# The dispatch scatters of a mixture-of-experts layer, paced by their landings

## The reference

```python
def _moe_forward(x, Wg, W1, W3, W2, Ws1, Ws3, Ws2):
    xt = x.reshape(-1, D)                                  # 2048 tokens x 512
    scores = jax.nn.softmax(xt @ Wg.T, axis=-1)
    ...                                                    # the best 2 of 4 groups, then the best 4 experts
    topi = jax.lax.top_k(masked, TOPK)[1]
    weights = jnp.take_along_axis(scores, topi, axis=1) * ROUTE_SCALE
    combine = jnp.zeros((T, E), xt.dtype).at[jnp.arange(T)[:, None], topi].add(weights)
    h = jax.nn.silu(jnp.einsum('td,eid->eti', xt, W1)) * jnp.einsum('td,eid->eti', xt, W3)
    expert_out = jnp.einsum('eti,edi->etd', h, W2)
    y = jnp.einsum('etd,te->td', expert_out, combine)
    z = jax.nn.silu(xt @ Ws1.T) * (xt @ Ws3.T) @ Ws2.T     # the shared experts
    return (y + z).reshape(B, S, D)
```

## Time and profile before

| what | value |
|---|---|
| median of 3 runs | 1945.23 us (1937.94 to 1947.1) |
| the profiled execution's own time | 1941.7 us |
| its span, first to last instruction | 1940.0 us |
| PE busy | 1519.6 us, 78% of the span |
| DVE busy | 1094.2 us, 56% |
| POOL busy | 685.1 us, 35% |
| ACT busy | 624.9 us, 32% |
| mean granted TensorE clock | 0.895 |

### The profile page before, as it was taken

How to read it: one execution, slowest core, us unless ns; L and a number is a source line. 1 busy time by engine, 2 the same in 40 slices (tenths; PEclk the granted TensorE clock), 3 DMA queues, 4 the chain that set the end, 5 groups by cost and what they waited for, 6 DMA issues and landing times. The chain is left out here.

```text
span 1940.0 us, 29164 instructions
## 1 busy us (share of the span) xinstructions
PE 1519.6 (78%) x9516; PEld 703.0 (36%) x9525; DVE 1094.2 (56%) x1809; ACT 624.9 (32%) x1103; POOL 685.1 (35%) x685
## 2 busy tenths in 40 slices
PE   1778787877167888888888748607999999999987
PEld 1344443434012222222222125203555555556443
DVE  6444444444568888988898376402344444444376
ACT  4312120303225666656666743001111111111121
POOL 3000000000545333333320024660364645666274
PEclk9989898998656899999999958858999999999999
DMA  4251607080344312222120012350566556573365
GB/s 173 55 195 36 214 14 235 0 249 8 105 126 138 66 34 47 53 47 47 28 56 1 1 47 93 151 195 11 180 177 157 163 146 173 159 200 87 114 189 179
DMA packets 183543, 211.00 MB, mean 109 GB/s; under 512 B 89968, under 2 KB 135600, under 8 KB 182960
## 3 DMA queue, kind: packets, MB, share of 16 engines
q1 hardware_dynamic: 154224, 123.73, 23.8%
q0 software_dynamic: 18592, 66.99, 11.1%
q10 hardware_dynamic: 10656, 19.40, 2.6%
HBM read 101.09 MB, written 88.87 MB: 98 GB/s over the span
## 5 line engine op out<-in xcount | busy, mean ns | idle before, releaser
L804 DVE TENSOR_REDUCE ca_mx<-ca_sc 128x1 f32<-128x512 f32 x512 | 327.6, 677 | 86.7 <-PE ca_sc L724 86.1
L77 PE MATMUL re_ab<-fx_w,re_xt 128*128 x1800 | 295.7, 314 | 10.9 <-DMA re_xt<-slot_rows 10.6
L937 ACT ACTIVATE ca_pt<-ca_st 128x512 f32<-128x512 f32 x512 | 264.5, 596 | 101.1 <-PE ca_st L736 101.1
L724 PE MATMUL ca_sc<-ca_ks,ca_qs 48*128 48x512 f16 x512 | 190.4, 424 | 53.7 <-DVE ca_mx L804 29.2
L77 PEld LDWEIGHTS re_ab<-fx_w,re_xt 128*128 128x128 f16 x1800 | 173.3, 98 | 109.0 <-issue 14.6
L736 PE MATMUL ca_st<-ca_qs,ca_ks 49*128 49x512 f16 x512 | 172.4, 400 | 40.6 <-ACT ca_pt L937 34.7
L77 PE MATMUL re_yp<-fx_w,re_ht 128*128 (+1 forms) x666 | 156.0, 379 | 0.0
L478 POOL TENSOR_TENSOR sa_yt<-sa_yf,sa_yt 128x512 f16<-128x512 f32 x16 | 18.5, 1156 | 385.8 <-ACT sa_yt L461 385.8
L1484 POOL TENSOR_TENSOR fx_w<-re_raw_w,fx_w 128x272 f16<-128x272 f32 x224 | 153.9, 723 | 1.7
L749 PE MATMUL ca_pv<-ca_pt,ca_va 128*32 128x512 f32 x1024 | 148.6, 645 | 1.0 <-DVE ca_turned L817 0.5
L77 PE MATMUL sh_yp<-sh_pair,sh_ht 128*128 128x512 f16 (+1 forms) x288 | 78.3, 430 | 77.6 <-DVE x_sb L1205 64.1
(11 more groups left out here) (236 smaller groups left out, 2432.3 us busy)
## 6 DMA issues: line engine op xcount, KB each, us to landing
re_raw_w<-in_we POOLq DMA_DIRECT2D x56, 544.0 KB, 4.6
slot_rows<-sa_zeros SPq DMA_DIRECT2D x12, 1792.0 KB, 16.0
slot_outs<-re_ys ACTq DMA_DIRECT2D x74, 256.0 KB, 2.0
sa_scratch<-sa_qk SPq DMA_DIRECT2D x16, 512.0 KB, 4.4
ca_scratch<-ca_qk SPq DMA_DIRECT2D x64, 128.0 KB, 1.8
sa_qs<-sa_scratch SPq DMA_DIRECT2D x12, 512.0 KB, 6.5
sa_ks<-sa_scratch SPq DMA_DIRECT2D x12, 512.0 KB, 6.8
ca_qs<-ca_scratch SPq DMA_DIRECT2D x48, 128.0 KB, 3.7
```

Of the source, the lines that this page charges most:

```text
L77: last = nc.tensor.matmul(out, lhs(a, c), rhs(b, c), start=(c == 0 and n == 0), stop=(c == chunks - 1 and n == len(PRODUCTS) - 1))
L724: nc.tensor.matmul(sc[:, m % RING, :], qs[rows, c % SLOTS, pair, qt * P:(qt + 1) * P], ks[rows, c % SLOTS, pair, :], start=True, stop=True ...
L804: nc.vector.reduce_max(mx[:, qd // 4, qd % 4, 2 * a + jj:2 * a + jj + 1], sc[:, m % RING, :], AX.X).then_inc(maxed, 1)
L937: nc.scalar.activation(pt[:, (4 * qd + k) % 8, :], st[:, m % RING, :], ACT.Exp, scale=SCALE).then_inc(exp_done, 1)
```

## The change

Two semaphores replace the one, and are used in turn. From the third scatter on, each waits until the scatter two places in front of it has landed (a landing adds 16). Two scatters at most are so under way at a time. At the end GpSimd waits for both counts. Nothing else is changed: size, order and number of the scatters are the same.

```diff
--- before.py
+++ after.py
@@ -1206,6 +1206,9 @@
                                      ALU.add).then_inc(self.added, 1)
 
 
+ABREAST = 2
+
+
 def route_and_share(nc, split, sems, ident, x_sb, xn, rows, route, wg_dram, we_dram, slot_rows, first_pairs):
 
 
@@ -1250,7 +1253,8 @@
         packed = sb("packed", [1, TILES], F32)
         made, logits_ready, shifted, exped, chain = (
             sem("made"), sem("logits_ready"), sem("shifted"), sem("exped"), sem("chain"))
-        masks_ready, placed, routed, sent = sem("masks_ready"), sem("placed"), sem("routed"), sem("sent")
+        masks_ready, placed, routed = sem("masks_ready"), sem("placed"), sem("routed")
+        sent = [sem(f"sent{n}") for n in range(ABREAST)]
         block = ctx.enter_context(nc.Block())
 
         @block.sync
@@ -1276,11 +1280,15 @@
                 shared.low_part(pool, nc.gpsimd, n)
 
             pool.wait_ge(routed, 1)
-            for t, k in sends:
+            for m, (t, k) in enumerate(sends):
+                if m >= ABREAST:
+                    pool.wait_ge(sent[m % ABREAST], 16 * (m // ABREAST))
                 nc.gpsimd.indirect_dma_start(
                     out=slot_rows, out_offset=bass.IndirectOffsetOnAxis(ap=route["index"][:, t, k:k + 1], axis=0),
-                    in_=rows[:, t, :, :].rearrange("p h d -> p (h d)"), in_offset=None).then_inc(sent, 16)
-            pool.wait_ge(sent, 16 * len(sends))
+                    in_=rows[:, t, :, :].rearrange("p h d -> p (h d)"), in_offset=None
+                ).then_inc(sent[m % ABREAST], 16)
+            for lane in sent:
+                pool.wait_ge(lane, 16 * len(sends) // ABREAST)
 
         @block.tensor
         def _(pe):
```

## The result

| | before | after |
|---|---|---|
| median of 4 runs each | 1943.2 us (1937.94 to 1947.1) | 1919.97 us (1909.45 to 1921.55) |
| profiled execution | 1941.7 us, span 1940.0 | 1920.77 us, span 1919.0 |

The ratio is 0.9866, with a 95% interval of 0.9827 to 0.9905: 1.3% faster. 1909 us was predicted, some 1.8% faster. 1920 us lies inside the stated range of 1899 to 1954 us, but outside the forecast's own range of 1900 to 1918.

The account below looks back on a forecast made before the run. It took late TensorE signals during the scatters as the bound: 1941.7 - 36.4 (earlier barrier) + 2.5 (cold start) = 1907.8 us, predicted as 1909 us after a small allowance for the median; range 1899 to 1954 us, the forecast's own 1900 to 1918.

Parts of the forecast that it names:

- What bounds the kernel: In the dispatch, TensorE's signals arrive late while scatters run back to back; this lateness, not the dispatch, bounds the stretch.
- the hole: TensorE's idle time of 47.88 us during outputs 1 in the dispatch, ended by a VectorE addition at 1313.45 us.
- the reads ended by "remote": ScalarE's reads of hidden 2's three units, 2.9, 8.5 and 52.4 us late, released by no work that had just finished.
- The signals get through: Gaps between paced scatters let TensorE's signals pass; TensorE ends near 1284 us, the barrier moves by -36.4 us.
- TensorE's 39.4 us: TensorE's work after hidden 2 without a hole: outputs 1, hidden 3, outputs 2 and 3, ending at 1284.4 us.
- The series: GpSimd's paced scatters in the dispatch: 2.85 us a pair, scatter 63 starting 88.4 us after scatter 1, scatter 64 1.4 later.
- The end of the stage: After scatter 64 starts at 1312.8 us: landing, 1.1 us for a slow scatter, 0.3 for the barrier; end about 1316.8.
- The cold start: TensorE idles from 1284 to about 1321 us and starts the routed experts at the low clock: 2.5 us added.
- Rival 1: Dispatch gaps too thin, the hole stays and everything behind moves 9.5 us later: 1951 us; chance 0.22.
- Rival 2: The dispatch pace itself is the bound, a pair needing 4.83 us: 1968 us; chance 0.06.
- Rival 4: The waits in the dispatch are over before GpSimd would start anyway, nothing changes: 1942 to 1945 us; chance 0.11.
- Rival 3: Half lifted: signals flow slower than TensorE makes them, TensorE ends after the dispatch, barrier near 1330: 1919 us; chance 0.16.

Follow-up runs that it names:

- e2: Kernel before, with GpSimd waiting at every eighth scatter until all earlier ones have landed, on chip A: ratio to before 0.9877 (0.9840 to 0.9915).
- e3: Kernel before, with a GpSimd memset of 0.30 us between scatters and no wait for a landing, on chip A: 1911.81 us.
- e1: Changed kernel with four semaphores, each scatter waiting for the landing four places in front instead of two, on chip A: 1945.64 us.
- e5: Kernel before, unpaced, each scatter moving only the high half of the rows to a tensor of its own, on chip A: 1945.32 us.
- e9: Kernel before, unchanged, run again on chip B: 1893.66 us.
- e12: Kernel before with a thin 128x16 memset of 0.13 us between scatters, on chip B: ratio to before 1.0016 (0.9991 to 1.0042).
- e8: As e2, but the wait for the last landings is on SyncE instead of GpSimd, on chip B: 1908.46 us.

## Why the prediction was right, and where it was off

*What bounds the kernel.* Right where the hole is: the reads ended by "remote" vanish with the hole in the changed kernel and in e2 and e3, and come back with it in e1 and e5. That TensorE had not been waiting for the scatters' data or for program code also holds: the data now lands later and TensorE ends earlier, and from 1223 to 1313 us e1 with its hole and e9 without one have two packets of program code each. One figure was misread: GpSimd's block had not been over for 46 us, but for 40.6, its DRAIN included.

*The signals get through.* Right, at an interval of 1.54 us; e2 and e3 show 1.47 and 1.48 to be enough. The prediction had argued for 1.42 us, between the gathers' 1.32 (late) and 1.47 (on time). No scatter series of the first comparison or of A had an interval between 1.33 and 1.47 us, so whether 1.42 would have been enough is open; that the pace came out slower, on the safe side, was luck. TensorE's 39.4 us from the start of outputs 1 measured 39.3 (1251.13 to 1290.44).

*The series.* The term was too small: 88.4 + 1.4 us were worked out from scatter 1 to 64, 96.8 measured, 7.0 more. The 2.85 us of a pair rested on the last packet, 2.4 us after its scatter's start; the trace after has 2.98 us, so that, with 0.3 for the start of the next, a landing is seen after 2.7. Over 31 pairs that is 4.0 us. The other 3 us are late scatters here and there, one with 2.1 us of idle time, which a paced series does not make good.

*The end of the stage.* This is the term that was mis-sized. From scatter 64 to the row reads 4.0 us were allowed: the landing, 1.1 for one slow scatter, 0.3 for the barrier. 8.5 were measured, and 5.3 of them are GpSimd's DRAIN. It was in the trace of before, and was overlooked since 40 us of slack lay over it. Together: 7.0 + 4.5 = 11.5 us, and the stage is 105.3 us where 93.8 was worked out.

*The cold start.* 2.5 us were added, and none is found: row reads to gather 1 is 0.7 us shorter than before. TensorE's first 36 matmuls are slower (7.74 us instead of 6.99 in the trace before), but there the routed experts wait for their row reads anyway.

*The sum.* 1907.8 us against 1920.8 of the profiled run. 11.5 of the 13.0 us are the two terms above; -2.5 for the cold start, +6.0 for the time ahead of scatter 1 and -2.1 for the rest make up what remains. Rivals 1, 2 and 4 are excluded in that comparison: reads on time, a landing of 2.7 us, scatters 1.54 us apart instead of 1.29. Rival 3 had named 1919 us, closer to the result than the forecast's 1909, but by chance: it wanted TensorE to end after the dispatch, and TensorE ends 35 us before scatter 64.

*What the prediction took for granted.* It treated the hole as a property of the program. The same program ran without it on B. On chip B the same argument with the hole left out gives the loss: series and tail cost 15 us that nothing pays for. None of the rivals was "there may be no hole to remove".

*The rule on contention* (the Trainium skill, SBUF — State Buffer, "Who interferes with whom": DMA never contends with a compute engine). As a statement on transfers it agrees with e5, where half the bytes changed nothing. Read as "pacing DMAs cannot help a compute engine", which it does not say, it would have been wrong by 25 us. No run here shows what in GpSimd's unbroken series of DMA instructions holds back TensorE's signals.

*What stays open.* Why B has no hole. Chip A was measured in one comparison only and B in three later ones, so that chip and time are not told apart; within each comparison the kernel before did not change sides (1934 to 1946 us in seven runs on A, 1893 to 1908 in thirteen on B). Whether a memset of 0.13 us, or a pause at every sixteenth scatter, suffices where there is one: they only ran on chip B. Whether mean interval or length of the unbroken run decides. No version here beat the kernel before on B; on A, e2 and e3 have stages 4 us shorter than the change had in the first result. The first to try on a chip with the hole is e12's memset, free on B, in the place of the waits, and with it e8's wait on SyncE. The gathers have not been paced: gather 1 to the end is 113.2 to 117.0 us in the six traces with late reads and 108.6 to 113.2 in the eight of B.

## What to carry to other kernels

When a wait is ended by a signal whose work had ended long before, the producer's signals are late: look for an engine that issues without a break at that time, and try to break its series. Here a short memset between the DMAs, a pause at every eighth and pacing by landings all did it, and all slowed the series; a break that costs nothing has not been shown to help. What a block's end costs behind the last instruction (here a DRAIN of 5.3 us and a landing of 2.7) is invisible while the engine has slack, and has to be added the moment the engine becomes the bound. And a gain that rests on removing a stall should be measured on more than one chip, beside the kernel before each time.

## What the runs showed that was not expected

- The same program takes 1934 to 1947 us in two comparisons and 1893 to 1908 us in three others on another chip, 2.4% apart by the medians. Between the traces of before and e9 it is 48.1 us: 40.8 in this one stall (stage 130.2 against 89.4 us) and 5.5 from gather 1 to the end, where signals are late too.
- TensorE's signals reach ScalarE up to 63.6 us late while the DMA engines are busy 27.2% of the time, and TensorE itself then issues a matmul only every 2.1 to 2.8 us (e5). VectorE's and ScalarE's signals are not late, and the last of TensorE's come through 5 us and more after the last packet (e1).
- A memset of 0.13 us between two indirect DMAs on GpSimd costs nothing measurable on B (1.0016, 0.9991 to 1.0042): it runs in the 0.30 us that pass between two such instructions anyway, 0.13 + 0.18 in e12.
- GpSimd's DRAIN at the end of this block takes 5.29 us behind the wait for the landing. With that wait on SyncE it runs beside the landing and ends 5.3 us after the last scatter's end (e8).
